# A softmax pipeline one slot deeper, and a state-space block with its intra-chunk products moved forward

## The reference

```python
x = L0_attn_x                       # 16 x 512 x 128
xn = _layernorm(x)
s = selective_scan(xn) in both directions, 16 states each      # "stage A"
g = silu(router_scale * mlp(xn))
x = x + s * g
xn = _layernorm(x)                                             # from here "stage B"
s = mamba2(xn)      # 4 chunks of 128: Y_diag (C.B * decay) x  +  Y_off from the carried states
g = silu(two layers of windowed attention + gated MLP (xn))    # 8 heads of 64, windows of 64
x = x + s * g
```

## Time and profile before

| | us |
|---|---|
| median of three runs | 4225.0 (4222.4 to 4226.27) |
| the profiled execution, its own time | 4227.29 |
| its span, first to last instruction | 4225.4 |
| TensorE's mean granted clock | 0.908 |
| PE / DVE / ACT / POOL busy | 3257.8 / 2527.5 / 2565.7 / 1720.2 |

### The profile page before, as it was taken

One profiled execution on the slowest core, in us unless ns is written; L12 is line 12 of the kernel. 1 busy time (PEld: TensorE's weight loads), 2 busy tenths in 40 slices (PEclk: granted clock), 3 DMA queues, 4 the chain that ended last, 5 costly groups with the idle time before them and its releaser, 6 DMA issues.

```text
span 4225.4 us, 57448 instructions
## 1 busy us (share of the span) xinstructions
PE 3257.8 (77%) x17248; PEld 1932.0 (46%) x17248; DVE 2527.5 (60%) x4239; ACT 2565.7 (61%) x5843; POOL 1720.2 (41%) x1428
## 2 busy tenths in 40 slices
PE   4677878787778777777787787777877777877776
PEld 2354444444445444444444445444444444545443
DVE  6565665656556565665656656575565655656543
ACT  4466666665666656566655666656666566565555
POOL 2353452535434353353533525244253542435332
PEclk9799999998989989898988989989899898999999
DMA  2000000000000000000000000000000000000000
GB/s 81 3 1 1 6 1 6 1 1 6 1 6 1 1 6 1 6 1 2 6 1 6 1 7 1 1 6 1 6 1 1 6 1 6 1 1 3 1 3 3
DMA packets 18387, 20.57 MB, mean 5 GB/s; under 512 B 768, under 2 KB 17152, under 8 KB 17792
## 3 DMA queue, kind: packets, MB, share of 16 engines
q1 hardware_dynamic: 18048, 16.44, 1.2%
HBM read 12.24 MB, written 4.19 MB: 4 GB/s over the span
## 4 chain that ended last, share of the span: by engine, by line
PE 39%; DVE 17%; issue 15%; ACT 14%; POOL 13%; DMA 0%; POOLq 0%; DVEq 0%; ACTq 0%; SPq 0%
PE bank L560 8%; PE bank L622 5%; ACT Pm L1044 5%; POOL hc L1446 4%; POOL oT L1513 4%; PE bank L798 3%; POOL oT L1505 3%; PE bank L782 3%; DVE tmp L1359 2%; DVE hst L1218 2%; PE bank L528 2%; DVE bank L1210 2%; DVE mx L1373 2%; PE bank L610 2%; PE bank L731 2%
## 5 line engine op out<-in xcount | busy, mean ns | idle before, releaser
L1446 POOL TENSOR_TENSOR hc<-hst,Cs 128x512 f32<-128x512 f32 x512 | 654.5, 1278 | 1086.8 <-DVE hst L1218 1021.7
L1218 DVE TENSOR_TENSOR_SCAN hst<-dA,bank 128x512 f32<-128x512 f32 x512 | 624.9, 1220 | 126.0 <-ACT dA L906 63.5
L560 PE MATMUL bank<-W,xs 128*128 128x512 f32 x960 | 498.7, 667 | 21.4 <-DVE tmp L1359 19.7
L912 ACT COPY Cs<-bank 128x512 f32<-128x512 f32 x512 | 299.3, 585 | 292.5 <-PE bank L543 262.4
L543 PE MATMUL bank<-parts,sel 96*128 96x512 bf16 x1024 | 352.9, 415 | 140.1 <-ACT Cs L912 66.0
L1044 ACT ACTIVATE Pm<-bank,mx 128x128 f32<-128x128 f32 x1024 | 362.7, 371 | 153.6 <-DVE mx L1373 153.6
L1520 POOL TENSOR_TENSOR Pm<-Pm,rinv 128x512 f32<-128x512 f32 x256 | 266.1, 1039 | 457.4 <-DVE rinv L1377 448.8
L1505 POOL TENSOR_TENSOR oT<-tmp 128x512 f32<-128x512 f32 x256 | 325.0, 1270 | 233.8 <-DVE tmp L1359 172.3
L1210 DVE TENSOR_TENSOR bank<-u,bank 128x512 f32<-128x512 f32 x512 | 349.9, 683 | 103.3 <-PE bank L543 102.3
L906 ACT ACTIVATE dA<-delta,neg_a 128x512 f32<-128x512 f32 x512 | 372.7, 728 | 49.1 <-DVE hst L1218 48.2
L528 PE MATMUL bank<-C,hc 128*128 128x128 f32 x2048 | 347.1, 297 | 38.5 <-POOL hc L1446 37.0
(11 more groups left out here) (223 smaller groups left out, 6287.9 us busy)
## 6 DMA issues: line engine op xcount, KB each, us to landing
W<-wpack SPq DMA_DIRECT2D x1, 4498.0 KB, 13.4
x_tok<-x SPq DMA_DIRECT2D x16, 256.0 KB, 2.9
out<-xa SPq DMA_DIRECT2D x16, 256.0 KB, 2.2
rot<-tables SPq DMA_DIRECT2D x2, 512.0 KB, 16.0
wc_f<-taps SPq DMA_DIRECT2D x1, 1024.0 KB, 19.4
C<-cpack SPq DMA_DIRECT2D x1, 721.0 KB, 14.6
Pm<-mask SPq DMA_DIRECT2D x1, 320.0 KB, 15.0
tmp<-rowpack SPq DMA_DIRECT2D x1, 256.0 KB, 17.3
```

What stands on the lines that cost most here:

```text
L560: mm(b[:, :], weights, rhs, start=True, stop=True).then_inc(full(ring, job), 1)
L1218: v.tensor_tensor_scan(o, a, b, 0.0, ALU.mult, ALU.add).then_inc(sem("a_h"), 1)
L1446: g_.tensor_tensor(hc[:, k % 2, :], hst[:, k % 2, :], Cs[:, k % 2, :], ALU.mult)\
```

## The change

**Softmax units.** The exponentials of unit n-1, its reciprocal and POOL's product now stand in the slot of unit n, beside that unit's maxima. On ACT they stand ahead of the copy of the transposed unit; they stood behind it. The transposes and the weighing keep their slots. The scores have banks 4 and 5 in turn, the transposed units bank 6 alone.

**State-space block.** Several yields are gone or moved, so that M (L1303 before) directly follows the mask, `xt0` and `xt1` directly follow `bt`, and `xdd` directly follows the three products on POOL. The copy `btok` on ACT is in slot 7 and the shifted copies in slot 8. PE's intra-chunk products of y0 (now in bank 7) stand ahead of the chunk states, those of y1 behind them, and only the carried ones are left for slot 9.

**Prologue.** `down(0)` and `down(1)` stand later on PE: stage B's slot comes between `up1` and `down(0)`.

```diff
-          + [(f"st{q}", "m_st", q + 1) for q in range(NT - 1)]
-          + [("y0", "m_y2", 1), ("y1", "m_y2", 2), ("yss", "m_yln", 1), ("mo", "m_sm1", 1)])
+          + [("y0", "m_y2", 1)] + [(f"st{q}", "m_st", q + 1) for q in range(NT - 1)]
+          + [("y1", "m_y2", 2), ("yss", "m_yln", 1), ("mo", "m_sm1", 1)])
...
+HOME |= {f"S{l}_{n}": n % 2 for l in range(NL) for n in range(NU)}
+HOME |= {f"PT{l}_{n}": 2 for l in range(NL) for n in range(NU)}
-HOME["G"] = OUT
+HOME |= {"G": OUT, "y0": OUT}
...
 # PE, prologue
                     if m == 2:
                         yield PRO + 6
+                        down(0)
...
-                    if m > 0:
-                        down(m - 1)
+                    if m == 3:
+                        down(1)
                 yield PRO + 7
+                down(2)
                 down(3)
 # PE, state-space block
                 for job, t in (("bt", 2), ("xt0", 0), ("xt1", 1)):
-                    if job == "xt0":
-                        yield 7
...
                 yield 8
+                pe.wait_ge(*step("m_M", i))
+                def within(g):
+                    pe.wait_ge(*step("m_xdt", i, g + 1))
...
+                within(0)
                 pe.wait_ge(*step("m_bt", i))
                 pe.wait_ge(*step("m_xdd", i))
...
+                within(1)
                 yield 9
-                pe.wait_ge(*step("m_M", i))
                 pe.wait_ge(*step("m_Ce", i))
                 pe.wait_ge(*step("m_st", i))
                 for g in range(2):
...
+                    carried(g)
 # ACT
-                yield 6
-                shifted(xs0, xn2, "t_xs", "m_xn", i, 1)
+                yield 7
                 act.wait_ge(*filled("B", "bt", i))
...
+                yield 8
+                shifted(xs0, xn2, "t_xs", "m_xn", i, 1)
...
+                        if 1 <= n < NU + 1:
+                            k = n - 1
+                            act.wait_ge(*step("t_max", i, NU * l + k + 1))
...
+                            b = bank("B", f"S{l}_{k}")
+                            for wi in range(4):
+                                last = f(Pm[:, k % 3, wi * P:(wi + 1) * P], b[:, wi * P:(wi + 1) * P], ACT.Exp,
+                                         bias=mx[:, k % 2, wi:wi + 1], accum_out=rsum[:, k % 2, wi:wi + 1])
+                            last.then_inc(sem("t_exp"), 1)
                         if LAG_T <= n < NU + LAG_T:
...
-                        if 0 <= n < NU:
-                            act.wait_ge(*step("t_max", i, NU * l + n + 1))
...
 # DVE
                 v.tensor_tensor(G, G, each(c("tri"), NT), ALU.mult).then_inc(sem("m_G"), 1)
-                yield 7
                 dve.wait_ge(*step("m_G", i))
...
-                            dve.wait_ge(*step("t_exp", i, NU * l + n + 1))
-                            if n >= 2:
-                                dve.wait_ge(*step("t_P", i, NU * l + n - 1))
-                            v.reciprocal(rinv[:, n % 2, :], rsum[:, n % 2, :]).then_inc(sem("t_rinv"), 1)
+                        if 1 <= n < NU + 1:
+                            k = n - 1
+                            dve.wait_ge(*step("t_exp", i, NU * l + k + 1))
+                            if k >= 2:
+                                dve.wait_ge(*step("t_P", i, NU * l + k - 1))
+                            v.reciprocal(rinv[:, k % 2, :], rsum[:, k % 2, :]).then_inc(sem("t_rinv"), 1)
 # POOL: yield 7 before xdd is gone; the product Pm*rinv is that of unit n-1
```

More of the change, by code:

```diff
@@ L649, in stage_b, with carried @@
                 yield 8
+                pe.wait_ge(*step("m_M", i))
+                def within(g):
+                    pe.wait_ge(*step("m_xdt", i, g + 1))
+                    if used("B", f"y{g}", i):
+                        pe.wait_ge(*vacant("B", f"y{g}", i))
+                    b = bank("B", f"y{g}")
+                    for q in range(NT):
+                        for hh in range(2):
+                            h = 2 * g + hh
+                            last = mm(b[hh * PM:(hh + 1) * PM, q * P:(q + 1) * P], xdt[:, q, h, :], big2[:, q, h, :],
+                                      start=(q == 0), stop=(q == 0), skip_group_check=True)
+                    return last
+                def carried(g):
+                    b = bank("B", f"y{g}")
+                    for q in range(1, NT):
+                        for hh in range(2):
+                            h = 2 * g + hh
+                            last = mm(b[hh * PM:(hh + 1) * PM, q * P:(q + 1) * P], st[:, q - 1, h, :], big1[:, q, h, :],
+                                      start=False, stop=True, skip_group_check=True)
+                    last.then_inc(full("B", f"y{g}"), 1)
+                within(0)
                 pe.wait_ge(*step("m_bt", i))
@@ L663, in stage_b @@
                 for g in range(2):
-                    if used("B", f"y{g}", i):
-                        pe.wait_ge(*vacant("B", f"y{g}", i))
-                    b = bank("B", f"y{g}")
-                    for q in range(NT):
-                        for hh in range(2):
-                            h = 2 * g + hh
-                            dst = b[hh * PM:(hh + 1) * PM, q * P:(q + 1) * P]
-                            last = mm(dst, xdt[:, q, h, :], big2[:, q, h, :], start=True, stop=(q == 0))
-                            if q > 0:
-                                last = mm(dst, st[:, q - 1, h, :], big1[:, q, h, :], start=False, stop=True)
-                    last.then_inc(full("B", f"y{g}"), 1)
+                    carried(g)
                 yield 10
@@ L1028, in stage_b @@
                                 .then_inc(sem("t_k"), 1)
+                        if 1 <= n < NU + 1:
+                            k = n - 1
+                            act.wait_ge(*step("t_max", i, NU * l + k + 1))
+                            if k >= 2:
+                                act.wait_ge(*step("t_rinv", i, NU * l + k - 1))
+                            if k >= 3:
+                                act.wait_ge(*filled("B", f"PT{l}_{k - 3}", i))
+                            b = bank("B", f"S{l}_{k}")
[3 more added lines that the diff above has]
+                            last.then_inc(sem("t_exp"), 1)
                         if LAG_T <= n < NU + LAG_T:
@@ L1035, in stage_b @@
                             nc.scalar.copy(PT[:, k % 2, :], b[:, :]).then_inc(sem("t_PT"), 1)
-                        if 0 <= n < NU:
-                            act.wait_ge(*step("t_max", i, NU * l + n + 1))
-                            if n >= 2:
-                                act.wait_ge(*step("t_rinv", i, NU * l + n - 1))
-                            if n >= 3:
-                                act.wait_ge(*filled("B", f"PT{l}_{n - 3}", i))
-                            b = bank("B", f"S{l}_{n}")
-                            for wi in range(4):
-                                last = f(Pm[:, n % 3, wi * P:(wi + 1) * P], b[:, wi * P:(wi + 1) * P], ACT.Exp,
-                                         bias=mx[:, n % 2, wi:wi + 1], accum_out=rsum[:, n % 2, wi:wi + 1])
-                            last.then_inc(sem("t_exp"), 1)
                         if LAG_V <= n < NU + LAG_V and (n - LAG_V) % 2 == 1:
@@ L1514, in stage_b @@
                                 prior.append(step("t_qk", i, k + 1))
-                        if 0 <= n < NU:
-                            k = n
+                        if 1 <= n < NU + 1:
+                            k = n - 1
                             pool.wait_ge(*step("t_rinv", i, NU * l + k + 1))
```

2 lines of the change are left out of this document (1 added, 1 removed).

## The result

| kernel | median, us | runs | ratio to before, 95% interval | profiled span, us |
|---|---|---|---|---|
| before | 4223.7 | 4 | 1 | 4225.4 |
| changed | 4154.5 | 4 | 0.9832 (0.9817 to 0.9848) | 4155.7 |

The change takes 69 us, 1.7% (70 between the two profiled executions). The forecast was 165 us, and 4154.5 lies 9.5 us outside its range. The direction held, the size didn't: `xdd` now starts 15 passes apart at 243.1 and 3984.9 us, which is 249.5 us a pass against 254.2 and 243 forecast.

What follows compares the result with a forecast made beforehand. No engine is full, so handoffs (waits between engines) were taken to bound the kernel. Gains of 58 + 48 + 56 + 3 (solo pass) = 165 us from 4227.3 gave 4062 us, range 3985 to 4145.

Steps and rivals of the forecast that it cites:

- State-space block: M starting at the mask's end brings the last y add 3.9 us sooner a pass; 58 us over 15 passes.
- Units of layer 0: Five softmax slots shorten by 0.8 us each, 4.0, less 0.8 for late first scores: 3.2 a pass, 48 in all.
- late first scores: First scores of each layer wait for the k copy, 2.3 us in layer 0; charged 0.8 there, 0.6 in layer 1.
- into slots that have a scan step at 1.9 us each anyway: Layer 0's last unit: its exponentials come a slot later, among slots already holding scan steps; charged nothing.
- POOL wait of the next slot: Layer 0: the next slot's transposes waited 1.56 us for POOL anyway, so late first scores were charged only 0.8.
- Layer 1 and prologue: Waits of 7.2 us go, less 2.6 for table loads and 0.6 for late scores: 4.0 a pass, 56 over 14.
- waits of 7.2 us: Layer 1's units: ACT's 4.3 us wait for maxima and the third and fourth gelu's 2.9 for `up` products both go.
- The rivals: Alternative outcomes: clock 0.15, layer 1 pays nothing 0.15, only the state-space block pays 0.08, slower 0.05, no effect 0.02.
- "slower" rival: Both layers' units: scores held until k and q copies, plus table loads, slots no shorter; 54 us more, 4281; chance 0.05.
- clock rival: State-space block and layer 1's units: granted clock rises from 0.80 to 1.00, 45 us more gain, 4017; chance 0.15.
- What would show each step: Signs of right: reciprocal's wait below 150 us, layer 0 maxima 3.4 to 3.6 apart, 28 more loads, pass about 243.
- a sign given for "wrong": PE's transposes waiting longer for copies than before was listed as showing the forecast wrong.

Runs made afterwards that it cites:

- e10_warm_yss: The changed kernel with ten added matmuls of constants in TensorE's wait ahead of the state-space block's sum of squares; 4125.0 us (0.9769).
- e5_gelus_late: The changed kernel with all four of the prologue's gelus behind layer 1's last exponentials, which removes the 28 further table loads; 4184.1 us (0.9898).
- e7b_own_bank_and_last_unit: The changed kernel with first scores in the values' bank and the last unit's exponentials in its own slot, both in both layers; 4096.5 us (0.9690).
- e16_with_warm: The changed kernel with first scores in the values' bank, layer 0's last unit unlagged, and constant matmuls ahead of sum of squares and first q/k transposes; 4091.7 us (0.9687).
- e1_ssm_only: The kernel before with only the state-space part of the change; 4183.1 us (0.9910).

## Why the prediction was wrong

**State-space block, -3.9 forecast, -2.55 measured (58 and 39 us).** The shift of M, `xdt`, `xdd` and the chunk states was right, and the y adds came even sooner. The step that failed is where I stopped: I took the shift at the last y add for that of the block. Behind it stand GpSimd's scan product and its two products in y (1.1 us of the shift gone in the pass shown: 4.5 to 3.4), and a wait of TensorE of 2.80 us with the half clock behind it (3.44 us for its four matmuls, not 2.47), which the trace of before had as 0.93 and 0.25 us. With the clock kept up there the block gets 3.7 of the 3.9 (25.39 to 21.66), but the stretches behind it give that back. By moving TensorE's products of y into an earlier wait the change opened a longer one later.

**Units of layer 0, -3.2 forecast, -0.9 measured.** The slots gave more than the 4.0 forecast (5.8) and the late first scores cost more than the 0.8 charged (1.85), which leaves 3.98 up to the last maxima for 3.2. But I charged nothing for the last unit, "into slots that have a scan step at 1.9 us each anyway". This is the term that failed: the drain is 3.1 us longer, 1.8 of it at full clock and 1.3 because TensorE, in ten passes of twelve, falls to half clock behind its new wait of 1.90 us for that unit's product. That the slots have work of their own was read as cover, though all of it is on the same engines' lists; in the last pass, which has no scan steps, `e10_warm_yss` has the late last unit and a drain of 10.49 us, as long as before (10.50). The run with the last unit in its slot in layer 0 has neither the wait nor the half clock there and gets 2.6 of the 3.1 back, 36 us.

**The late first scores** were charged at 0.8 and 0.6 us. The wait was read rightly as 2.3 us, but I set the POOL wait of the next slot against it, as hiding it. In layer 0 that wait hides nothing: an own bank gives 2.0 us. In layer 1 it gives only 0.45, for a reason that stays open. The last interval and the end, which I thought to gain, lose 6.6 us: in the last pass the first maxima come 2.4 (layer 0) and 5.4 us (layer 1) later, of which the slots get 3.8 and 3.4 back, and layer 1's drain is 2.6 longer in each of the two passes. That last loss is not the late unit's but the clock's: `e10_warm_yss` has the same late unit and 10.5 us in both.

**Layer 1 and prologue, -4.0 forecast, -3.0 measured.** Nearest to right, but not by its terms. The waits of 7.2 us and the loads of 2.6 were to leave 4.6, less 0.6 for late scores; measured are 2.22 in the drain and 0.77 before it. The first maxima come 4.2 us later, not 0.6, and the way from them to the last is 5.0 shorter. That a sum of waits on two engines is a gain of the pass was the error, and that the total comes within 1.0 is in part luck.

**The rivals.** None was it. The "slower" rival named the right mechanism, scores held by copies, at 2.3 and 2.8 us, but wrongly had the slots pay nothing. The clock rival was right that the granted clock of the block and of layer 1's units rises (0.81 to 0.89, 0.89 to 0.96), but it fell in layer 0 and ahead of layer 1's first maxima, and TensorE's busy time as a whole rose 27 us. Per pass the shortfall is 1.35 (block), 2.3 (layer 0) and 1.0 (layer 1) of 11.1 us. By the masks, the first 14 intervals were to give about 155 us and gave 79 (3601.7 to 3522.9; the first two of them 2.5 together, not looked into); the start, the last interval and the end were to give the other 10 and cost 9.

What would show each step was met for the reciprocal (85 us), the chunk states (4.0 us sooner) and the 28 loads, and nearly for M (0.13 us behind the mask's end, not 0.1); the maxima came closer together than said (3.0 to 3.5, not 3.4 to 3.6). It was missed for the pass (249.5, not 243). Near to a sign given for "wrong" are TensorE's new waits for copies; they stand ahead of its scores, not of its transposes.

Open: why `e5_gelus_late` lets TensorE wait up to 4.4 us for the gelu was read from the order on ScalarE, not tried (3.5 us in `e7b_own_bank_and_last_unit` lie within the 2.7 to 4.3 of before). A filled wait in layer 1's projections wasn't tried either, nor the `down` order taken out of the changed kernel.

## What to carry to other kernels

Lagging one step of a pipeline by a slot pays in the steady slots and is paid for at both ends: price the fill (what the first item's buffer is held by) and the drain (the last item has no next one to stand beside) from the rows there and not at nothing: here 1.85 and 3.1 us a pass in layer 0, against 5.8 gained between. Try the last item unlagged; here that paid in layer 0 and not in layer 1. Follow a shift to the last instruction of the stretch, past every engine's list, and ask of TensorE's moved products which wait they leave empty. Give the lag and the buffers that it needs together: here each alone cost 2% to 5%.

## What the runs showed that was not expected

The same matmuls behind the same waits take different times from kernel to kernel. Take six projection matmuls of layer 1, about 42 us behind `wo` of layer 0. In two kernels they stand behind waits of TensorE of 3.13 and 1.20 us; first the kernel before, then `e7b_own_bank_and_last_unit`:

```profile
2161.75 3.95 PE L560 MATMUL bank<-W,xs 128*128 128x512 f32 x6
```

```profile
2103.83 5.40 PE L564 MATMUL bank<-W,xs 128*128 128x512 f32 x6
```

In `e16_with_warm`, with matmuls added just ahead, they take 2.83:

```profile
2102.32 2.83 PE L568 MATMUL bank<-W,xs 128*128 128x512 f32 x6
```

The granted clock over the six is 0.50, 0.71 and 1.00 in `e7b_own_bank_and_last_unit`, before and `e16_with_warm`, and 5.40 us is near twice 2.83: they run wholly at half clock in one kernel, partly in another. The same holds between passes of one kernel: in `e1_ssm_only` the stretch from the y adds to the block's end is 9.54 to 9.59 us in four of passes 3 to 15 and 11.07 to 11.22 in the other nine, with nothing between; where it is short, so is the next stretch (25.97 against 27.3). A forecast of a local edit in this kernel has that much scatter per stretch, some 1.3 to 2.6 us in the places shown, whatever its own size.
